# Layer-2 field products in four row strips, a y bank in its turn, and W2 loaded with h on the partitions

## The reference

```python
x_vec = input                                   # (512, 64, 16)
for W, b in params:                             # W0 (128, 64*64), W1 and W2 (128, 128*64)
    z = jnp.einsum('bhd,bfd->bhfd', x_vec, input)
    B, h, f, d = z.shape
    z = z.reshape(B, h * f, d)
    x_vec = jnp.einsum('oc,bcd->bod', W, z) + b[None, :, None]
    outs.append(x_vec.sum(axis=2))
return jnp.concatenate(outs, axis=1)            # (512, 384)
```

## Time and profile before

| | |
|---|---|
| median of 3 runs | 1092.18 us (1091.85 to 1092.72) |
| the profiled execution, its own time | 1091.6 us |
| its span, first to last instruction | 1089.5 us |
| mean granted TensorE clock | 0.997 |
| TensorE, VectorE, ScalarE, GpSimd busy | 98%, 81%, 65%, 79% |

### The profile page before, as it was taken

How to read it: one execution, slowest core, us unless ns; L and a number is a source line. 1 busy time by engine, 2 the same in 40 slices (tenths; PEclk the granted TensorE clock), 3 DMA queues, 4 the chain that set the end, 5 groups by cost and what they waited for, 6 DMA issues and landing times.

```text
span 1089.5 us, 18056 instructions
## 1 busy us (share of the span) xinstructions
PE 1064.6 (98%) x4783; PEld 803.5 (74%) x4783; DVE 877.3 (81%) x2673; ACT 710.3 (65%) x2447; POOL 859.6 (79%) x727
## 2 busy tenths in 40 slices
PE   5999999999999999999999999999999999999997
PEld 5777777777778777777778777777778877777676
DVE  5768989889874888989894798989886598888881
ACT  4666767676764767767673676777675576767770
POOL 2668997989884897989985799898987589898550
PEclk9999999999999999999999999999999999999998
DMA  7942423332322323323241232433332133320000
GB/s 275 245 92 81 101 71 71 96 76 78 66 70 58 76 78 69 85 57 97 66 87 40 56 97 66 88 84 69 94 79 59 47 69 97 76 79 28 1 23 8
DMA packets 108327, 85.88 MB, mean 79 GB/s; under 512 B 71040, under 2 KB 73824, under 8 KB 108096
## 3 DMA queue, kind: packets, MB, share of 16 engines
q1 hardware_dynamic: 106832, 78.17, 29.3%
q10 hardware_dynamic: 1392, 6.55, 1.9%
HBM read 14.75 MB, written 0.79 MB: 14 GB/s over the span
## 4 chain that ended last, share of the span: by engine, by line
PE 90%; DVE 3%; ACT 2%; DMA 2%; POOL 1%; issue 1%; ACTq 0%; SPq 0%; DVEq 0%; POOLq 0%
PE y L913 62%; PE l L934 9%; PE l L913 8%; PE xt L1021 5%; PE l2p L1033 4%; DVE acc L769 2%; DMA gram<-in_L_rec_W_dram 1%; PE l2p L1010 1%; ACT y L662 1%; DMA z<-xg 1%; ACT prod L673 1%; POOL z L453 1%; DVE gram L851 1%; PE l L922 0%; POOL pacc L463 0%
## 5 line engine op out<-in xcount | busy, mean ns | idle before, releaser
L769 DVE SCALAR_TENSOR_TENSOR acc<-y,x0t,acc 128x128 f32<-128x128 f32 x2048 | 559.8, 341 | 101.8 <-PE y L913 99.1
L673 ACT ACTIVATE prod<-y,x0t 128x128 f32<-128x128 f32 x1280 | 365.8, 379 | 157.4 <-PE y L913 148.6
L913 PE MATMUL y<-w1h,x1h 128*128 128x512 f32 x1024 | 464.6, 454 | 2.2 <-DVE acc L769 1.4
L913 PE MATMUL y<-w1h,x1l 128*128 128x512 f32 x1024 | 402.1, 393 | 0.0
L913 PE MATMUL y<-w1l,x1h 128*128 128x512 f32 x1024 | 400.6, 391 | 0.0
L453 POOL TENSOR_TENSOR z<-z,xg 128x512 f32<-128x512 f32 (+2 forms) x272 | 352.5, 1300 | 32.8 <-DMA z<-xg 32.8
L463 POOL TENSOR_TENSOR pacc<-pacc,prod 128x512 f32<-128x512 f32 x192 | 268.0, 1396 | 79.7 <-ACT prod L673 78.3
L913 PEld LDWEIGHTS y<-w1h,x1h 128*128 128x128 f32 x1024 | 193.2, 189 | 96.8 <-issue 26.5
L662 ACT ACTIVATE y<-y,x0t 128x128 f32<-128x128 f32 x512 | 142.6, 342 | 157.4 <-PE y L913 157.2
L913 PEld LDWEIGHTS y<-w1l,x1h 128*128 128x128 f32 x1024 | 192.8, 188 | 59.3 <-issue 28.8
L913 PEld LDWEIGHTS y<-w1h,x1l 128*128 128x128 f32 x1024 | 192.1, 188 | 43.0
(11 more groups left out here) (85 smaller groups left out, 673.0 us busy)
## 6 DMA issues: line engine op xcount, KB each, us to landing
z<-xg SPq DMA_DIRECT2D x480, 128.0 KB, 2.4
w2t<-in_L_rec_W_dram SPq DMA_DIRECT2D x8, 512.0 KB, 7.1
gram<-in_L_rec_W_dram ACTq DMA_DIRECT2D x8, 512.0 KB, 7.4
xg<-in_r_input_dram SPq DMA_DIRECT2D x30, 128.0 KB, 3.8
z<-xg SPq DMA_DIRECT2D x32, 96.0 KB, 5.9
z<-xg SPq DMA_DIRECT2D x15, 192.0 KB
gram<-in_L_rec_W_dram ACTq DMA_DIRECT2D x1, 2048.0 KB, 9.2
out_dram<-z SPq DMA_DIRECT2D x4, 192.0 KB, 1.9
```

Source lines behind the costliest of these rows:

```text
L673: last = nc.scalar.activation(prod[:, h % HSLOTS, k, :], y[c % YB][:, k * O:(k + 1) * O], ACT.Copy, scale=x0t[:, j, f:f + 1])
L769: ins = nc.vector.scalar_tensor_tensor(out=to, in0=of, scalar=x0t[:, j, f:f + 1], in1=b1r[:] if m == 0 else to, op0=ALU.mult, op1=ALU.add)
L913: ins = nc.tensor.matmul(to, stationary, moving, start=(first and k == 0), stop=(last and k == 2))
```

## The change

The field products go in four strips of 32 rows with 2 batch elements each, 2 x 64 + 2 = 132 columns, into four banks: the two of l2p, a part of xt's bank (now `spare`), and one of the four y banks. The y bank is taken in turn: a tile now has 17 turns (16 chunks and, behind chunk 12, the product), and each turn waits for the user of the bank four turns back, so chunk 13 waits for chunk 10 (before: 9), 14 for 11, 15 for 12, the next tile's chunk 0 for `layer2_out`, and the product itself for chunk 9. The product also waits until xt and l2 in the shared bank have been read. `layer2_out` takes six copies instead of two; `own_rows` makes two scalings instead of four. The turn of x goes from chunk 28 to chunk 34. W2 is loaded by ScalarE's queue in the second group, 8 parts at chunks 4, 11, ... 53, straight from memory with h on the partitions (pieces of 64 elements); its turns and their copies go, the first layer-2 product comes at chunk 28, and the quarters read W2 as `w2t[:, :, f]`.

```diff
-HALF = P // 2
-HALF_B = TILE_B // 2
+STRIPS = 4
+STRIP = P // STRIPS
+STRIP_B = TILE_B // STRIPS
-GRAM = HALF_B * F
+GRAM = STRIP_B * F
-TURN_AT = LAYER2_AT + CHUNKS
+TURN_AT = LAYER2_AT + CHUNKS + 6
-W2_LOAD_AT = [k * 3 // 2 for k in range(W_PARTS)]
+W2_LOAD_AT = [4 + 7 * k for k in range(W_PARTS)]
-        w2t = sb("w2t", [P, F, O])
+        w2t = sb("w2t", [P, O, F])
-        xt = ps("xt", [P, TILES, F])
-        l2 = xt[:].rearrange("p t f -> p (t f)")[:, 0:QB]
+        spare = ps("spare", [P, CHUNK])
+        xt = spare[:, 0:TILES * F].rearrange("p (t f) -> p t f", f=F)
+        l2 = spare[:, 0:QB]
+        l2p_spare = spare[:, TILES * F:TILES * F + GRAM + STRIP_B]
+        def turn_of(j, c):
+            return (CHUNKS + 1) * j + c + (1 if c > LAYER2_AT else 0)
+        def ybank(j, c):
+            return turn_of(j, c) % YB
+        def l2p_bank(j):
+            return l2p_turn(j) % YB
+        def l2p_turn(j):
+            return (CHUNKS + 1) * j + (LAYER2_AT + 1 if j < TILES else 0)
 # layer2_out (ScalarE)
-                nc.scalar.copy(gram[:, :, bass.ds(to, TILE_B)].rearrange("p f (k b) -> p f k b", k=2),
-                               l2p[:, :, 0:GRAM].rearrange("p k (b f) -> p f k b", f=F))
-                nc.scalar.copy(sums1[:, bass.ds(tile * TILE_B, TILE_B)].rearrange("p (k b) -> p k b", k=2),
-                               l2p[:, :, GRAM:GRAM + HALF_B]).then_inc(l2p_used, 1)
+                own_bank = y[l2p_bank(j)]
+                for at, of, k in ((0, l2p[:], 2), (2, l2p_spare.unsqueeze(1), 1), (3, own_bank[:].unsqueeze(1), 1)):
+                    b = at * STRIP_B
+                    nc.scalar.copy(gram[:, :, bass.ds(to + b, k * STRIP_B)].rearrange("p f (k b) -> p f k b", k=k),
+                                   of[:, :, 0:GRAM].rearrange("p k (b f) -> p f k b", f=F))
+                    last = nc.scalar.copy(
+                        sums1[:, bass.ds(tile * TILE_B + b, k * STRIP_B)].rearrange("p (k b) -> p k b", k=k),
+                        of[:, :, GRAM:GRAM + STRIP_B])
+                last.then_inc(l2p_used, 1)
 # load_w2 (ScalarE's queue, now in group 1)
-                    act.wait_ge(w0l_made, W0_STEPS - 1)
-                part = slice(k * F * O // W_PARTS, (k + 1) * F * O // W_PARTS)
-                act.dma_start(w2raw[:, part], w2[:, part]).then_inc(w2_loaded, 16)
+                    act.wait_ge(w1_turned, CHUNKS)
+                part = slice(k * O // W_PARTS, (k + 1) * O // W_PARTS)
+                act.dma_start(w2t[:, part, :], w2[part, :].rearrange("o (h f) -> h o f", f=F)).then_inc(w2_loaded, 16)
-                for b in range(HALF_B):
+                for b in range(STRIP_B):
 # TensorE; turn_w2 and w2_out are gone
-                    last = nc.tensor.matmul(l2, w2t[:, f, :], gram[:, f, :], start=(f == 0), stop=(f == F - 1))
+                    last = nc.tensor.matmul(l2, w2t[:, :, f], gram[:, f, :], start=(f == 0), stop=(f == F - 1))
+            def turn_free(tile, j, turn):
+                user, c = turn_ahead(tile, j, turn)
+                if c is None:
+                    pe.wait_ge(l2p_used, user + 1)
+                elif c in HELPED:
+                    pe.wait_ge(prod_made, HN * user + HN + HELPED.index(c) + 1)
+                else:
+                    pe.wait_ge(acc_step, added(user, c))
 # layer2
-                for k in range(2):
-                    half = slice(k * HALF, (k + 1) * HALF)
-                    last = nc.tensor.matmul(l2p[:, k, 0:GRAM + HALF_B], x2[half, slot], bd[half, slot, :],
+                turn_free(tile + 1, j, l2p_turn(j))
+                pe.wait_ge(x0t_made, fields_kept)
+                pe.wait_ge(l2_used, quarters_out)
+                for k, to in enumerate((l2p[:, 0], l2p[:, 1], l2p_spare, y[l2p_bank(j)][:])):
+                    rows = slice(k * STRIP, (k + 1) * STRIP)
+                    last = nc.tensor.matmul(to[:, 0:GRAM + STRIP_B], x2[rows, slot], bd[rows, slot, :],
                                             start=True, stop=True)
 # chunk
+                turn_free(tile, j, turn_of(j, c))
 # at TURN_AT
                         pe.wait_ge(x0t_made, 2 * n + 2)
+                        pe.wait_ge(l2p_used, n * TILES + 2)
```

More of the change, by code:

```diff
@@ L341, in pool_at, with turn_ahead @@
             return POOL_STEPS * tile + (POOL_STEPS + 1 + step)
+        def turn_of(j, c):
[6 more added lines that the diff above has]
+            return (CHUNKS + 1) * j + (LAYER2_AT + 1 if j < TILES else 0)
+        def turn_ahead(tile, j, turn):
+            back, at = divmod(turn - YB, CHUNKS + 1)
+            if at == LAYER2_AT + 1:
+                if isinstance(tile, int) and tile - j + back < 1:
+                    return turn_ahead(tile, j, turn - YB)
+                return tile - j + back, None
+            return tile - j + back, at - (1 if at > LAYER2_AT else 0)
         FIRST, LAST = slice(0, TILES - 1), slice(TILES - 1, TILES)
@@ L603, in body @@
                         w1_upper(e + W1_AHEAD)
-                    if kind == "first" and e in W2_LOAD_AT:
+                    if n == 1 and e in W2_LOAD_AT:
                         load_w2(W2_LOAD_AT.index(e))
@@ L617, in body @@
                         scale(tile, j, c)
-                    if kind == "first" and W2_AT <= e - 1 < W2_AT + CHUNKS:
-                        w2_out(e - 1 - W2_AT)
-                    if c == layer2_at(n, j) + 1 and (kind != "first" or j > 0):
+                    if c == LAYER2_AT + 1 and (kind != "first" or j > 0):
                         before = (n * TILES + (j - 1) + QG * TILES) % (QG * TILES) if kind != "first" else j - 1
-                        layer2_out(tile - 1, before * TILE_B)
+                        layer2_out(tile - 1, j, before * TILE_B)
                     if e == QUARTER_AT[-1] + 1 and kind == "inner":
@@ L1002, in turn_row @@
                 last.then_inc(turned, 1)
[L1004 to L1012, removed]
             def quarter(q, part, fields_kept):
@@ L1037, in chunk @@
             def chunk(tile, j, c):
[L1039 to L1044 removed]
+                turn_free(tile, j, turn_of(j, c))
                 cols = slice(j * P, (j + 1) * P)
[L1046 removed]
+                by_parts(y[ybank(j, c)][:], x1h[:, cols], x1l[:, cols], w1h[:, c, :], w1l[:, c, :],
                          True, True, True).then_inc(y_made, 1)
@@ L1089, in body @@
                         turn_row(ROWS_AT.index(e))
-                    if kind == "first" and W2_AT <= e < W2_AT + CHUNKS:
-                        if e == W2_AT:
-                            pe.wait_ge(w2_loaded, 16 * W_PARTS)
-                        turn_w2(e - W2_AT)
-                    if c == layer2_at(n, j) and (kind != "first" or j > 0):
-                        if kind == "first" and j == 1:
-                            pe.wait_ge(w2_kept, CHUNKS)
-                        layer2(tile - 1, (j - 1) % 2)
+                    if c == LAYER2_AT and (kind != "first" or j > 0):
+                        fields_kept = 2 * n + (3 if j == TILES - 1 and kind != "last" else 2)
+                        layer2(tile - 1, (j - 1) % 2, j, fields_kept, (n - (j == 0)) // QG + 1)
                     if e in QUARTER_AT and kind == "inner":
```

57 lines of the change are left out of this document (22 added, 35 removed).

## The result

The changed kernel takes 1150.24 us (median, 1149.62 to 1150.9), the kernel before, run beside it, 1092.45 (1091.85 to 1093.49): a ratio of 1.0528, 95% interval 1.051 to 1.0546. That is 58 us more, where 17 were forecast. The profiled execution has a span of 1147.9 us at a mean granted clock of 0.996.

The account below looks back on a forecast made before the run. The prediction took TensorE's queue as the bound from the second group to the last but one. Its terms, 4 + 1 + 5 - 11 + 0.5 + 17.4 = +17 us on a median of 1092.2, gave 1109 us, range 1091 to 1120.

Parts of the forecast that it names:

- the price of W2's new layout: Quarters of the layer-2 contraction: strided weight loads at 0.146 us against 0.112 set the pace, 512 x 0.034 = +17.4 us.
- Tile 1 has more still: Chunk 14's wait for VectorE's chunk 11: tile 1 has more than tile 2's 0.46 margin, so keeps its 0.2 gain.
- the turn of x alone: Turn of x at chunk 34: costs 0.59 alone against 0.24 beside the product, +0.35 in 14 groups, +5 us.
- the strips' 0.20: Layer-2 field products on TensorE: four strips run side by side, 0.61 us for 0.83, a gain of 0.2 each.
- tile 0's gain turned into a wait: Tile 0, chunk 14: no margin after VectorE's chunk 11, so the 0.2 gain becomes a wait; +0.1 us per group.
- tile 3's wait: Tile 3, chunk 14: TensorE waits 0.3 to 0.4 us more for VectorE's chunk 11; +0.45 per group.
- the loads of W2: W2's loads in the second group on ScalarE's queue: +0.5 us, with two more pairs of copies; bounds 0 and 4.
- First group: Without W2's 16 turns on TensorE the first group shortens: -11 us, bounds -8 and -15.
- the hidden load: Rival at the four quarters: the strided load stays hidden, the 17.4 us are gone, 1092 us; 13%.
- the strips in series: Rival at layer-2 products: strips run one behind the other, each product costs 0.45 more, 1131 us; 8%.
- the free bank turns: Rival: the turn of banks never bites, VectorE coming earlier with TensorE; -11 in place of +5, 1093 us; 6%.
- the 15 us from the first group: Rival: W2 frees the 15 us in full, together with free bank turns; about 1089 us; 3%.

Follow-up runs that it names:

- W2 alone: The kernel before with only W2 loaded in the second group in its new layout, no turns of W2, quarters reading with step 64: 1132.31 us, ratio 1.0362.

## Why the prediction was wrong

The side was right, the size not: 1150 lies 30 us beyond the range.

- **The step that failed** is the last of the sum, the price of W2's new layout. "The trace has that pattern in the same tile: the turns of W1 read it with a step of 64." Tile, step and number of columns were the same; the instruction wasn't. The turns are transposes, one load and one pass each; the quarter's are full-precision matmuls. Mixed in one kernel they go at 0.133 and 0.208 a load. "512 x 0.034 = +17.4" measured 48.1, and that is 30.7 of the 41 us by which the forecast was short. Its mechanism, that the load sets the pace, was right.
- **The bound on it failed with it.** "Bounds 0 and 17.4" took the nearest row for the upper end. A row of another kind of instruction isn't an end; nothing in the trace excluded a higher price, and the range should have had room above.
- **The second step that failed** is "Tile 1 has more still". The margin of each tile was VectorE's end in the old trace against TensorE's start in the old trace, and for chunk 14 alone; chunk 13 against chunk 10 was not compared, and the wait came there. In tile 1 an instruction of VectorE has a length that goes with GpSimd's phase, 0.69 or 1.80 us, and it had its short length in the old trace. A gain of 0.2 became a wait of 0.63. In group 6, from the last chunk matmul ahead of each product to the second matmul behind the wait, tile 1 alone is 0.7 worse than forecast (+0.51 for -0.2); the other three and the turn of x are within 0.1. With the turn of x, the 14 groups measured +17.4 for the +9.5 forecast; moving that one subtraction gives 0.7% back. Why GpSimd and VectorE meet in that phase now wasn't settled; the turn of x alone doesn't do it.
- **Right:** the strips' 0.20 and all four side by side; tile 0's gain turned into a wait; tile 3's wait (0.44 for 0.3 to 0.4); the turn of x alone (0.60 for 0.59, +6 for +5); the loads of W2 at next to nothing. Without that subtraction in the way, strips, banks and turn take the ratio from 0.9918 to 0.9999, some 9 us, where the sum had 10; that is partly luck, since the first group gave 1.4 of it where the sum had nothing, and the last one 2.1 where it had 1.
- **First group:** W2 alone gave -11.1 with the later start counted (-11.5 without), as the sum had it. In the full change -9.2 remain, counted in the same way. This group has three products too, and the sum had bank turns in the 15 others only: between 26 and 110 us TensorE waits 1.2 us for VectorE's acc and 0.4 for the copies of a product (`layer2_out`), and with W2 alone for neither. The granted clock is also lower there, 0.95 between 26 and 60 us where W2 alone had 1.00. What each is worth wasn't tried apart.
- **Small:** a strip has 130 columns (2 x 64 + 2), not 132; the eight instructions of a product took 0.50 for 0.45; the last group cost 2.1 for 1.
- **Rivals:** the hidden load is refuted by each quarter, the strips in series by the timeline, the free bank turns by tiles 1 and 3, and with them the 15 us from the first group, which gave 11 at most.

## What to carry to other kernels

A price read from another instruction in the same tile is only an estimate until the kind of instruction agrees as well: the pace of a full-precision matmul's loads doubled from a step of two to four values, where a transpose's was still the same at a step of eight. If a new layout saves transposes once but puts a step into a stationary operand that is read many times, copying it straight once is cheaper: without strips that was the difference between 1.0362 and 0.9918. And where a change shortens a chain of waits by one buffer, compare every chunk that loses a buffer, and ask of each releaser whether its own length goes with what another engine does at that moment.

## What the runs showed that was not expected

- The price of a strided load is a step and not a slope: 0.106, 0.114, then 0.221, 0.226, 0.207, 0.208 us at steps 1, 2, 4, 8, 16, 32.
- Four strips of 32 rows in four banks run side by side: the four of a pass start within 0.02 us, and the eight matmuls of a product lie between 457.12 and 457.62.
- Sixteen strided loads took 3.32 us at a granted clock of 0.50 as at 1.00, where contiguous loads with their matmuls went from 0.10 each to 0.20.
